# A decoder layer's mixer on one core: projections from high and low parts, rows turned between their halves, and both weighings of the output at the end of a period

## What is computed

```python
xn = _layernorm(x, ln_gamma, ln_beta)
k = jnp.einsum('btc,dc->btd', xn, Wk)
v = jnp.einsum('btc,dc->btd', xn, Wv)
r = jnp.einsum('btc,dc->btd', xn, Wr)
td = jax.nn.sigmoid(time_decay)
tf = jax.nn.sigmoid(time_first)
kv = k * v
weighted_kv = kv * jnp.power(td[None, None, :], t_idx)
csum = jnp.cumsum(weighted_kv, axis=1)
shifted = jnp.concatenate([zeros, csum[:, :-1]], axis=1)
wkv = tf * kv + td * shifted
out = jnp.einsum('btc,dc->btd', jax.nn.sigmoid(r) * wkv, Wo)
x = _layernorm(x + out)
```

## Time and profile before

| what | value |
|---|---|
| median of 3 runs | 2179.31 us (2178.28 to 2179.53) |
| profiled execution, its own time | 2181.61 us |
| span of its profile | 2179.8 us |
| TensorE busy | 2008.5 us, 92% of the span |
| DVE busy | 1572.4 us, 72% |
| POOL busy | 1491.9 us, 68% |
| ACT busy | 1228.6 us, 56% |
| mixer stage | about 13 to 275.7 us of the span |

### The profile page before, as it was taken

The page is one execution under the profiler, slowest core; times in us unless marked ns, Lnnn a source line. Parts: engine busy times, 40 slices in busy tenths (PEclk is TensorE's granted clock), DMA queues, the critical chain, the costliest instruction groups (busy, mean ns, idle before and its releaser), DMA issues. The chain is left out here.

```text
span 2179.8 us, 51607 instructions
## 1 busy us (share of the span) xinstructions
PE 2008.5 (92%) x14104; PEld 1753.8 (80%) x14104; DVE 1572.4 (72%) x3671; ACT 1228.6 (56%) x3408; POOL 1491.9 (68%) x1707
## 2 busy tenths in 40 slices
PE   5999869999999999976999999999999999387798
PEld 2555548888888788765999999999999999276687
DVE  3666536877878778764777778888888888167976
ACT  3555446666666656632777777777777777132231
POOL 2666521577766777663777778888888888285765
PEclk9999979999999999998999999999999999699899
DMA  4300013233242332403677767777767777244752
GB/s 129 97 0 0 0 43 127 79 123 112 78 155 78 105 127 77 141 25 126 218 233 235 242 218 231 234 235 233 239 231 233 232 232 232 109 181 174 234 172 87
DMA packets 244901, 329.86 MB, mean 151 GB/s; under 512 B 50074, under 2 KB 167234, under 8 KB 244836
## 3 DMA queue, kind: packets, MB, share of 16 engines
q1 hardware_dynamic: 218788, 279.97, 39.7%
q0 software_dynamic: 26048, 49.10, 6.1%
HBM read 236.17 MB, written 77.18 MB: 144 GB/s over the span
## 5 line engine op out<-in xcount | busy, mean ns | idle before, releaser
L1191 POOL DMA_INDIRECT slot_token<-a_entry,a_slot_i x256 | 262.9, 1027 | 113.8 <-issue 71.4
L1687 POOL DMA_INDIRECT part_rows<-e_out,e_dest x184 | 210.9, 1146 | 74.1 <-issue 67.1
L1820 ACT ACTIVATE e_sg<-e_g 128x256 f32<-128x256 f32 x368 | 142.0, 386 | 203.6 <-PE e_g L1512 202.5
L1679 POOL DMA_INDIRECT e_xg<-x_rows,e_tok x188 | 196.6, 1045 | 84.0 <-issue 56.3
L1869 DVE TENSOR_TENSOR e_h<-e_sg,e_u 128x256 f32<-128x256 f32 x368 | 158.0, 429 | 98.6 <-PE e_u L1512 39.6
L1011 ACT ACTIVATE a_prob<-a_s,a_ntop 128x128 f32<-128x128 f32 x512 | 180.9, 398 | 0.6 <-DVE a_ntop L1382 0.5
L1695 POOL TENSOR_TENSOR e_wd1l<-e_raw_d,e_wd1h 128x256 fp32r<-128x256 f32 x184 | 145.4, 823 | 17.2 <-ACT e_wd1h L1800 16.4
L1695 POOL TENSOR_TENSOR e_wd0l<-e_raw_d,e_wd0h 128x256 fp32r<-128x256 f32 x184 | 146.0, 827 | 14.3 <-ACT e_wd0h L1800 13.5
L1884 DVE TENSOR_SCALAR e_out<-e_d,e_dest 128x256 f32<-128x256 f32 x184 | 80.7, 480 | 102.3 <-PE e_d L1512 102.3
L1512 PE MATMUL e_d<-e_wd1h,e_ht1h 128*128 128x256 f32 x368 | 109.3, 297 | 24.6 <-issue 24.6
L866 PE MATMUL a_o<-a_wo,a_ot 128*128 128x256 f32 x512 | 123.5, 385 | 7.9 <-DVE a_ot L1449 7.9
(11 more groups left out here) (330 smaller groups left out, 7537.9 us busy)
## 6 DMA issues: line engine op xcount, KB each, us to landing
e_raw_g<-in_eg SPq DMA_DIRECT2D x94, 512.0 KB
e_raw_u<-in_eu SPq DMA_DIRECT2D x94, 512.0 KB, 5.5
e_raw_d<-in_ed SPq DMA_DIRECT2D x93, 512.0 KB, 5.0
part_rows<-a_zero SPq DMA_DIRECT2D x16, 2048.0 KB, 9.3
f_part<-part_rows SPq DMA_DIRECT2D x16, 2048.0 KB, 10.1
x<-in_x SPq DMA_DIRECT2D x16, 512.0 KB, 3.6
x_rows<-x SPq DMA_DIRECT2D x16, 512.0 KB
out_rows<-f_res SPq DMA_DIRECT2D x16, 512.0 KB, 3.4
```

The costliest lines, as they stand in the source:

```text
L1191: pool.indirect_dma_start(k.slot_tok, bass.IndirectOffsetOnAxis(ap=slot_i[:, j, q:q + 1], axis=0), entry[:, j, q, :], None, bounds_check=S ...
L1679: pool.indirect_dma_start(xg[a][:, n, :], None, k.x2_d, bass.IndirectOffsetOnAxis(ap=tok[a][:, n, 0:1], axis=0))\
L1687: pool.indirect_dma_start(k.part_d, bass.IndirectOffsetOnAxis(ap=dest[a][:, n, 1:2], axis=0), out[a][:, n, :], None).then_inc(put[a], 16)
L1820: act.activation(sg[m % 2][:], bank_g[m % 2][:, 0:SETW], ACT.Silu).then_inc(sg_rdy, 1)
```

## The change

The gamma of the norm goes into the weights, and its beta into an offset for each output column. At the start ACT writes the high parts of the six weight chunks times gamma in float32r (`weights_high`), DVE the low parts (`weights_low`), and TensorE makes Wk, Wv and Wr times beta in twelve products of one column (`offsets`). The offsets then come in as bias of `keys` and `gate`, and for the values in `keyed`, which becomes a scalar_tensor_tensor. A group's turned rows are copied by ACT as high part, and DVE subtracts it from the bank for the low part (`turned_low`). `project` calls `split_product` with six products a bank. xnt and y have two buffers each, chosen by the parity of the group, so the hardware loop now holds two periods. TensorE turns group g + 1 between the halves of the projection and weighs both halves of group g - 1 last. ACT, POOL and DVE run norms, rstd and moments one group further ahead, and DVE does both residuals and the outgoing moments of group g - 2 first. ve, nm, rs and off count on one semaphore. All code outside the mixer is the same.

```diff
         w = {n: p.sb("w" + n, [P, DC, D]) for n in "kvro"}
-        xn, xnt = p.sb("xn", [P, TG, D]), p.sb("xnt", [P, DC, GW])
+        parts = {n: [p.sb(f"w{n}{h}", [P, DC, D], F32R) for h in "hl"] for n in "kvr"}
+        offset = {n: p.sb("b" + n, [P, DC]) for n in "kvr"}
+        xn, xnt = p.sb("xn", [P, TG, D]), [[p.sb(f"xnt{i}{h}", [P, DC, GW], F32R) for h in "hl"] for i in range(2)]
...
-        run, y = p.sb("run", [P, DC, GW]), p.sb("y", [P, DC, GW])
+        run, y = p.sb("run", [P, DC, GW]), [p.sb(f"y{i}", [P, DC, GW]) for i in range(2)]
...
+
+            period(0, 0)
+            period(1, 1)
+            with eng.Fori(1, NG // 2 - 1) as i:
+                period(2 * i, 0)
+                period(2 * i + 1, 1)
+            period(NG - 2, 0)
+            period(NG - 1, 1)
...
-                            pe.wait_ge(xnt_rdy, ONE + DC * (g - 1) + c + 1)
+                            pe.wait_ge(xl_rdy, ONE + DC * (g - 1) + c + 1)
...
-                        pe.wait_ge(xnt_rdy, ONE + DC * (g + 1))
+                        pe.wait_ge(xl_rdy, ONE + DC * (g + 1))
...
-                        for q in range(DC):
-                            last = pe.matmul(bank[:], w[n][:, q, c * P:(c + 1) * P], xnt[:, q, :],
-                                             start=(q == 0), stop=(q == DC - 1))
-                        last.then_inc(kvr_done, 1)
-
-                def mix(g, h):
+                        high, low = parts[n]
+                        cols = slice(c * P, (c + 1) * P)
+                        split_product(pe, bank[:], [((high[:, q, cols], low[:, q, cols]), (xnt[par][0][:, q, :], xnt[par][1][:, q, :]))
+                                                    for q in range(DC)]).then_inc(kvr_done, 1)
...
-                            last = pe.matmul(bank_o[h][:, (j % 2) * D:(j % 2 + 1) * D], y[:, q, j * T:(j + 1) * T],
...
+                            last = pe.matmul(bank_o[h][:, (j % 2) * D:(j % 2 + 1) * D], y[par][:, q, j * T:(j + 1) * T],
...
-                def period(g):
-                    project(g, 0)
-                    if at_least(g, 1):
-                        mix(g - 1, 0)
-                    project(g, 1)
+                def period(g, par):
+                    project(g, par, 0)
                     if more(g):
                         turn(g + 1)
+                    project(g, par, 1)
                     if at_least(g, 1):
-                        mix(g - 1, 1)
-
+                        mix(g - 1, 1 - par, 0)
+                        mix(g - 1, 1 - par, 1)
+
...
-                pe.wait_ge(w_in, DMA + 64)
+                pe.wait_ge(low_rdy, ONE + LOWS)
...
-                def turned(g):
-                    act.wait_ge(kvr_done, ONE + 3 * DC * g)
+                def turned(g, par):
+                    if at_least(g, 2):
+                        act.wait_ge(kvr_done, ONE + 3 * DC * (g - 1))
                     for c in range(DC):
                         act.wait_ge(t_done, ONE + DC * g + c + 1)
-                        act.activation(xnt[:, c, :], bank_t[c][:], ACT.Identity, bias=k.bet[:, c:c + 1],
-                                       scale=k.gam[:, c:c + 1]).then_inc(xnt_rdy, 1)
+                        act.activation(xnt[par][0][:, c, :], bank_t[c][:], ACT.Copy).then_inc(xnt_rdy, 1)
...
-                    act.activation(kc[:, c, :], bank_k[:], ACT.Copy).then_inc(kc_rdy, 1)
+                    act.activation(kc[:, c, :], bank_k[:], ACT.Identity, bias=offset["k"][:, c:c + 1]).then_inc(kc_rdy, 1)
...
-                    act.activation(sr[:, c, :], bank_r[:], ACT.Sigmoid).then_inc(sr_rdy, 1)
+                    act.activation(sr[:, c, :], bank_r[:], ACT.Sigmoid, bias=offset["r"][:, c:c + 1]).then_inc(sr_rdy, 1)
...
-                def period(g):
+                def period(g, par):
                     keys(g, 0)
                     gate(g, 0)
                     if more(g):
-                        norm_in(g + 1)
+                        turned(g + 1, 1 - par)
                     keys(g, 1)
+                    if more(g, 2):
+                        norm_in(g + 2)
+                    gate(g, 1)
                     if at_least(g, 2):
                         norm_out(g - 2)
-                    gate(g, 1)
-                    if more(g):
-                        turned(g + 1)
+
...
+                def weights_high():
+                    act.wait_ge(w_in, DMA + 64)
+                    for n in "kvr":
+                        for c in range(DC):
+                            act.activation(parts[n][0][:, c, :], w[n][:, c, :], ACT.Identity, scale=k.gam[:, c:c + 1])\
+                               .then_inc(high_rdy, 1)
...
                 norm_in(0)
-                turned(0)
+                weights_high()
+                turned(0, 0)
+                norm_in(1)
+                act.wait_ge(low_rdy, ONE + LOWS)
...
+                    pool.wait_ge(rs_s, ONE + 4 * g + 2)
                     pool.tensor_tensor(rs_t[:], ve_t[:], k.mhalf[:], ALU.pow).then_inc(rs_s, 1)
-                    pool.wait_ge(rs_s, ONE + g + 1)
-                    pool.tensor_tensor(off_t[:], nm_t[:], rs_t[:], ALU.mult).then_inc(off_s, 1)
+                    pool.wait_ge(rs_s, ONE + 4 * g + 3)
+                    pool.tensor_tensor(off_t[:], nm_t[:], rs_t[:], ALU.mult).then_inc(rs_s, 1)
...
-                def gated(g, c):
+                def gated(g, par, c):
                     pool.wait_ge(wkv_rdy, ONE + DC * g + c + 1)
                     pool.wait_ge(sr_rdy, ONE + DC * g + c + 1)
-                    pool.wait_ge(o_done, ONE + 2 * g)
-                    pool.tensor_tensor(y[:, c, :], run[:, c, :], sr[:, c, :], ALU.mult).then_inc(y_rdy, 1)
-
-                def period(g):
-                    if more(g):
-                        rstd_in(g + 1)
+                    if at_least(g, 2):
+                        pool.wait_ge(o_done, ONE + 2 * (g - 1))
+                    pool.tensor_tensor(y[par][:, c, :], run[:, c, :], sr[:, c, :], ALU.mult).then_inc(y_rdy, 1)
+
+                def period(g, par):
                     decayed(g, 0)
                     if at_least(g, 2):
                         rstd_out(g - 2)
+                    if more(g, 2):
+                        rstd_in(g + 2)
                     decayed(g, 1)
-                    gated(g, 0)
-                    gated(g, 1)
+                    gated(g, par, 0)
+                    gated(g, par, 1)
 
...
-                    dve.tensor_tensor(kv[:, c, :], kc[:, c, :], bank_v[c][:], ALU.mult).then_inc(kv_rdy, 1)
+                    dve.scalar_tensor_tensor(kv[:, c, :], bank_v[c][:], offset["v"][:, c:c + 1], kc[:, c, :],
+                                             ALU.add, ALU.mult).then_inc(kv_rdy, 1)
...
+                def weights_low():
+                    for i, n in enumerate("kvr"):
+                        for c in range(DC):
+                            dve.wait_ge(high_rdy, ONE + DC * i + c + 1)
+                            dve.scalar_tensor_tensor(parts[n][1][:, c, :], w[n][:, c, :], k.gam[:, c:c + 1],
+                                                     parts[n][0][:, c, :].bitcast(F32), ALU.mult, ALU.subtract)\
+                               .then_inc(low_rdy, 1)
...
+                    dve.wait_ge(off_done, 1)
+                    for i, n in enumerate("kvr"):
+                        dve.tensor_copy(offset[n][:], bank_o[0][:, i * DC:(i + 1) * DC]).then_inc(low_rdy, 1)
...
+                def turned_low(g, par):
+                    for c in range(DC):
+                        dve.wait_ge(xnt_rdy, ONE + DC * g + c + 1)
+                        dve.tensor_tensor(xnt[par][1][:, c, :], bank_t[c][:], xnt[par][0][:, c, :].bitcast(F32),
+                                          ALU.subtract).then_inc(xl_rdy, 1)
...
-                def period(g):
+                def period(g, par):
                     if at_least(g, 2):
+                        residual(g - 2, 0)
                         residual(g - 2, 1)
+                        moments_out(g - 2)
+                    keyed(g, 0)
+                    if more(g, 2):
+                        moments_in(g + 2)
+                    summed(g, 0)
+                    keyed(g, 1)
                     if more(g):
-                        moments_in(g + 1)
-                    keyed(g, 0)
-                    if at_least(g, 2):
-                        moments_out(g - 2)
-                    summed(g, 0)
-                    if at_least(g, 1):
-                        residual(g - 1, 0)
-                    keyed(g, 1)
+                        turned_low(g + 1, 1 - par)
                     summed(g, 1)
...
                 moments_in(0)
+                moments_in(1)
+                weights_low()
+                turned_low(0, 0)
+                dve.wait_ge(low_rdy, ONE + LOWS)
```

## The result

The changed kernel takes 2184.13 us (median of 14, 2181.19 to 2186.67), the kernel before 2179.24 (median of 14). The ratio is 1.002, with a 95% interval of 1.0012 to 1.0029: slower by 4.9 us, where the forecast was 2176.5 us and 2.8 less. The time lies in the range that was given, 2162 to 2190; the sign is the other one. A repetition of it later gave a ratio of 1.0015 (1.0007 to 1.0024).

A forecast was written before the change was run, and what follows sets the result against it. TensorE bound the kernel before; after the change the DVE and POOL loop would. Terms +1.9, -2.6, -5.9, +3.0, +0.2, +0.6 sum to -2.8: 2178.8 us profiled, 2176.5 median, range 2162 to 2190.

The forecast's parts named there:

- The mechanism: Mixer loop: DVE and POOL hold each other up and set 14.9 us a period, TensorE waiting some 2.4 us in each.
- the walk: Once round the mixer's DVE and POOL chain, from kv of half 0 to the next: 14.9 us, bounds 14.4 and 15.2.
- a branch each second period about 0.1: Last step round the DVE and POOL loop: the hardware loop's branch adds about 0.1 us before the next kv.
- periods 4 to 13: Mixer groups in which the DVE and POOL loop rules: ten periods 0.3 us longer each, +3.0 us.
- periods 1 to 3: Early mixer groups in which TensorE still sets the pace: 38.0 us for 43.9, -5.9 us.
- drain: End of the mixer, last groups in a row as before: +0.6 us for the last kv behind the outgoing moments.
- The start: Before the mixer's first product: ScalarE's high parts of the weights move it from 25.99 to 27.9, +1.9 us.
- No hold: Rival in the mixer loop: DVE and POOL don't hold each other, TensorE's 12.5 us rules, near 2145 us; 9%.
- the scan ahead of y: Rival in the mixer loop: DVE's scan starts before POOL's y, 1.1 us a period less, 2165 us; 9%.
- ScalarE ahead of the gate: Rival, something else on the chain: ScalarE's norms ahead of the gate hold TensorE, some 1 us a period, 2187; 6%.
- The new forms holding POOL: Rival: DVE's new kv form and low parts stretch POOL's rstd, +0.7 us a period, 2184, up to 2190; 13%.
- The clock: Rival: TensorE's clock falls because it now waits; at half rate over 60 us more, above 2240 us; 3%.

The follow-up runs named there:

- before_two_y: The kernel before with only a second y buffer and the loop over pairs of groups it needs: 2181.21 us, ratio 1.0004 to the kernel before.
- high_only: The changed kernel with two matmuls of high parts a bank instead of six, products with low parts left out: 2176.40 us (one run).

## Why the prediction went wrong

- *The mechanism* was right, but for one of its reasons: a loop of two engines that hold each other, in both directions, with y ahead of the scan each time, TensorE waiting and at full clock. Its links came at 5.50 (predicted 5.5), 7.48 (7.4), 11.09 (11.0) and 13.33 (13.2) behind kv. The reason that it gave for y being ahead, "with two y it follows the decay directly", doesn't hold for this change: with one y the scan is held as well (15.32). It is the new order, in which both weighings of the group before have ended by then. Only in the old order is it the second buffer (before_two_y).
- *The failed step* is the last one of the walk, "a branch each second period about 0.1", and with it 14.9. The same program without the loop gives 14.93 to 14.95; with it 15.33. The loop form (branch and registers) costs 0.38 a period, not 0.1, part of it through a race: by 0.11 us or less a small operation of POOL gets ahead of a scan or is caught. The term of periods 4 to 13 was +3.0 and is +7.0: 4.0 of the 6.5 us by which the stage's sum was off. About 2.8 of the 4.0 are the loop form; the other 1.2 are small excesses along the rest of the walk, which came to 14.95 without the loop where 14.8 had been added up.
- *Smaller terms*, all too favourable: periods 1 to 3 -4.9 for -5.9 (the slow loop begins at 13.75 in period 3, and a matmul takes 0.233 for 0.227), period 0 -1.8 for -2.6, drain +1.3 for +0.6. Period 14 was +0.2 as predicted. The start was +2.0 for +1.9, and that was luck. The sum had ScalarE last and said that the one-column products "lie beside this and cost nothing". The rows of the changed kernel show them ahead of the transposes on TensorE:

```profile
22.90 1.84 PE L320 MATMUL m_o<-bet,m_wr 128*128 128x1 f32 x8
24.61 1.95 PE L277 MATMUL m_t<-ident,m_xn 128*128 128x128 f32 x8
...
25.74 0.60 ACT L348 ACTIVATE m_xnt0h<-m_t 128x512 fp32r<-128x512 f32 x1 [0.48 <-PE m_t L277]
```

  The transposes start at 24.61, 23.11 before, though the norm had ended at 22.86. ScalarE was through with its high parts by 25.25, not 26.1, and then waited for the transposes. What the start would be without these products wasn't run.
- *Rivals.* No hold, and the scan ahead of y: no; 2.28 and 0.08 behind y in each period. ScalarE ahead of the gate: TensorE does wait for m_sr (13.2 us in 11 times, from 60 to 240 us), but with 5.6 us of TensorE's work gone on both sides of this wait the period stays (15.17), and with the hold of the scan gone, ScalarE's order untouched, it falls to 14.22. The new forms holding POOL: in the rows above, ve takes 0.23 beside a low part (139.99) and rs 1.04 beside kv in its new form (154.09), the unheld lengths. The Trainium skill (SBUF — State Buffer, Who interferes with whom) says that a DVE instruction with at most one SBUF input, outside the 2-port modes, does not contend with GpSimd, and the trace agrees for these two forms, by the 0.23 and 1.04 just named. The clock: unchanged here, but it fell in two experiments.
- *The chances.* The walk had 14.9 for likeliest with bounds of 14.4 and 15.2, the upper one with ve caught. 15.33 is above them: ve was caught in every second period only, but no bound allowed for a dearer loop. A sum that ends within 3 us of zero has no sign to speak of: without the 4.0 of this one term the stage would have come out even, 0.3 under the one before. That the unrolled kernel comes out 3.2 us under the one before, near the 2.8 forecast, is in part luck: its stage is only 1.6 shorter. The terms of the first period and the drain rest on the rows alone; no run took them apart.

## What to carry to other kernels

When an engine gets faster, walk once round the next loop and look which of two neighbours' instructions meet: here an instruction of one engine cost the other 1 us in each period, and starting it later alone gave 14.5 us back, moving work from between the two decays behind them 23. With both, and a norm of ScalarE moved that had become the next link, most of what the change had been built for came through (2151 us). Check such a walk for races of 0.1 us and for the price of the hardware loop, which a sum of durations doesn't contain. Where a change has several parts, ask of each whether the order leaves it anything to do: the second y buffer did nothing in this one, and in the old order it only made scans slower.

## What was not expected of the hardware

- TensorE's granted clock: behind an idle stretch of 2.74 us in each period matmuls came 0.43 us apart, the lower level (1.2 GHz), at a granted clock of 0.50 from 150 to 153 us, and 0.23 again from 153.5 on; behind 1.54 us the clock stayed at 1.00. So a wait that lengthens can cost more than itself (1.25 us a period here). In high_only it was 0.73 of full from 60 to 240 us, where TensorE was busy for 121.90 of the 180.
- A hardware loop over two groups costs 0.4 us in each period of 15 here, where two engines are bound to each other (15.33 with it, 14.95 without). f32r matmuls of 128x512 with another weight each time start 0.233 us apart (141.31 to 143.41 in the changed kernel, nine steps).
- The holds are the same in all runs: in the slow periods a scan takes 2.27 to 2.31 where y started 0.07 to 0.09 ahead of it, and 1.22 to 1.25 else.
